# SyncE's order of edge-attribute loads, index loads and waits in the convolution phase of a two-layer graph network

## The reference, cut to what matters

```
filters  = silu(edge_attr @ fW1 + fb1) @ fW2 + fb2      # edge_attr: 206250 x 50
messages = (h[src] @ dW + db) * filters                 # h: layer norm and relu of x, 6250 x 128
aggregated = segment_sum(messages, dst, 6250)
x = x + (h + silu(aggregated @ uW1 + ub1) @ uW2 + ub2)
```

## Time and profile before

| | us |
|---|---|
| median of 3 runs (5270.76 to 5274.32) | 5273.22 |
| the profiled execution, its own time | 5256.96 |
| its span in the trace, first to last instruction | 5255.3 |
| TensorE busy in the span (matmuls) | 3757.2 |
| GpSimd busy | 3117.0 |
| VectorE busy | 2361.3 |
| ScalarE busy | 1582.3 |
| convolution over the edges, start of gathers to start of the node update | 2684 to 5228 |

### The profile page before, as it was taken

How to read it: one execution, slowest core, us unless ns; L and a number is a source line. 1 busy time by engine, 2 the same in 40 slices (tenths; PEclk the granted TensorE clock), 3 DMA queues, 4 the chain that set the end, 5 groups by cost and what they waited for, 6 DMA issues and landing times. The chain is left out here.

```text
span 5255.3 us, 54906 instructions
## 1 busy us (share of the span) xinstructions
PE 3757.2 (71%) x14371; PEld 2737.0 (52%) x14372; DVE 2361.3 (45%) x5579; ACT 1582.3 (30%) x4766; POOL 3117.0 (59%) x3258
## 2 busy tenths in 40 slices
PE   7666666666666666666747767776767677777868
PEld 5444444444444444444546555565655556656656
DVE  6566666666666666666652222222222222222223
ACT  4455445555445555455420010000100100010001
POOL 4666666666666666666455565656556656665653
PEclk9555555555555555555575566656566655565567
DMA  2222222222222222222122222222222222222222
GB/s 79 46 45 45 45 45 44 44 45 45 45 45 44 45 44 45 46 45 44 40 76 58 55 60 59 57 59 61 55 59 59 57 59 60 57 60 59 57 59 62
DMA packets 150585, 277.69 MB, mean 53 GB/s; under 512 B 77209, under 2 KB 91489, under 8 KB 146054
## 3 DMA queue, kind: packets, MB, share of 16 engines
q0 software_dynamic: 104064, 218.11, 17.7%
q1 hardware_dynamic: 46290, 58.74, 4.0%
q10 hardware_dynamic: 200, 0.48, 0.0%
HBM read 267.31 MB, written 9.73 MB: 53 GB/s over the span
## 5 line engine op out<-in xcount | busy, mean ns | idle before, releaser
L57 POOL DMA_INDIRECT ce_xg<-table,ce_idx x1612 | 1527.0, 947 | 1003.2 <-DVE ce_msg L1211 516.2
L57 POOL DMA_INDIRECT ae_xg<-table,ae_idx x1612 | 1538.9, 955 | 936.7 <-issue 467.7
L1138 ACT ACTIVATE ce_hid<-ce_ps_h,ce_fb 128x768 f32<-128x768 f32 x269 | 242.2, 901 | 2288.5 <-remote 1542.5
L1179 PE MATMUL ce_ps_h<-ce_ea,ce_fw 50*128 50x384 f32 x1076 | 669.3, 764 | 322.8 <-ACT ce_hid L1138 168.6
L1208 DVE TENSOR_TENSOR ce_ps_f<-ce_ps_f,ce_fb 128x768 f32<-128x768 f32 x269 | 259.2, 963 | 1409.7 <-remote 1046.4
L1158 PEld LDWEIGHTS ce_ps_f<-ce_fw,ce_hid 128*128 128x128 f32 x3228 | 638.1, 293 | 399.8 <-issue 377.1
L1158 PE MATMUL ce_ps_f<-ce_fw,ce_hid 128*128 128x128 f32 x3228 | 728.3, 397 | 146.6 <-issue 146.1
L654 PE MATMUL ae_ps_k<-ae_xg,ae_e 128*96 128x129 f32 x3224 | 832.2, 430 | 1.1 <-ACT ae_e L567 1.1
L654 PEld LDWEIGHTS ae_ps_k<-ae_xg,ae_e 128*96 128x96 f32 x3224 | 685.4, 278 | 46.8 <-issue 45.5
L1167 PE MATMUL ce_ps_a<-ce_hot,ce_msg 128*128 128x32 f32 x3224 | 569.0, 332 | 194.1 <-issue 193.9
L1167 PEld LDWEIGHTS ce_ps_a<-ce_hot,ce_msg 128*128 128x128 f32 x3224 | 588.2, 272 | 195.2 <-issue 195.1
(11 more groups left out here) (144 smaller groups left out, 3204.2 us busy)
## 6 DMA issues: line engine op xcount, KB each, us to landing
ce_ea<-in_edge_attr SPq DMA_DIRECT2D x90, 450.0 KB
ae_xg<-table,ae_idx POOLq DMA_INDIRECT x1612
ce_xg<-table,ce_idx POOLq DMA_INDIRECT x1612
table<-pr_rows POOLq DMA_DIRECT2D x7, 462.0 KB, 4.1
pr_x<-in_x SPq DMA_DIRECT2D x7, 448.0 KB, 3.3
table<-fa_hd SPq DMA_DIRECT2D x7, 448.0 KB, 3.0
out_x<-y SPq DMA_DIRECT2D x7, 448.0 KB, 3.0
fa_x<-in_x SPq DMA_DIRECT2D x6, 448.0 KB, 4.0
```

Of the source, the lines that this page charges most:

```text
L57: eng.indirect_dma_start(out=out, out_offset=None, in_=table[:, :], in_offset=bass.IndirectOffsetOnAxis(ap=idx, axis=0)).then_inc(done, 16)
L1138: nc.scalar.activation(hid[:, b, :].rearrange("p (k e) -> p k e", k=2), ps_h[:, :].rearrange("p (k e) -> p k e", k=2)[:, :, 0:H], ACT.Silu ...
L1179: last = nc.tensor.matmul(ps_h[:, k * 512:k * 512 + H], fw1[:, :], ea[:, s // LOAD, q:q + H], start=True, stop=True)
```

## The change: what it does

`load_indices` takes a function that issues the attribute load, and calls it at another place and with another turn. Before, load k stood ahead of the wait for the gathers of group k and the index load of group k+2. Now both attribute loads of the first turn stand at the very start, and in each group of turn i the attribute load of turn i+1 follows the index load. So load k+2 comes right behind the wait for the gathers of group k. The last turn issues no attribute load. There are 90 attribute loads and 92 index loads, as before, with the same waits, buffers and sizes. The attention stage calls `load_indices` without the function and issues what it issued before. No other engine's program changes.

```diff
-def load_indices(sp, a, h, idx, idx_in, gathered, landed, also=lambda r, i, v: None):
+def load_indices(sp, a, h, idx, idx_in, gathered, landed, ahead=lambda r, i, v: None):
...
         def following(i):
             for v in range(LOADS):
-                also(r, i, v)
                 read(r, i, v)
                 sp.dma_start(idx[v][:, :],
                              a["src"][bass.ds((i + 1) * LOADS + v, 1), :, 0:P // 2, :].rearrange("u o p c -> (u o) p c")).then_inc(idx_in[v], 16)
-
+                ahead(r, i + 1, v)
+
+        for v in range(LOADS):
+            ahead(r, 0, v)
         following(0)
         with sp.Fori(1, TURNS - 1) as i:
             following(i)
         for v in range(LOADS):
-            also(r, TURNS - 1, v)
             read(r, TURNS - 1, v, REST)
             sp.dma_start(idx[v][:, :], a["src"][v, :, 0:P // 2, :]).then_inc(idx_in[v], 16)
```

## The result

The changed kernel took 5295.01 us (median of 6, 5287.97 to 5303.38), the kernel before on the same chip 5273.77 us (6 runs, 5269.71 to 5279.64). The ratio is 1.0039, interval 1.0028 to 1.0051: 21 us slower. The forecast was 5268 us and no change that can be told; 5295.01 us lies at the upper end of the range (5295).

A forecast was written before the change was run, and what follows sets the result against it. The prediction took the convolution to be paced between GpSimd and TensorE, with SyncE outside that loop. Steady loads 0, index loads 0 and start -5 us turned 5273.2 into 5268 us, range 5239 to 5295.

The forecast's parts named there:

- What bounds the phase: Convolution: no engine full; GpSimd pauses 6.0 us per group for TensorE's chain, 28.14 us per group, no SyncE instruction involved.
- (a): Convolution's attribute loads 2 to 89: 60 go out some 6 us earlier, but nobody waits for them; 0 us.
- bounds of -23 to +43: Best and worst for the steady loads, in us, from stretches of 27.75 and 28.86 us per group over 60 groups.
- the forecast's own sign of being wrong: Convolution's steady pace off 28.14 us by over 0.2 us per group, with GpSimd's pause or its filter-step distance changed.
- 28.24 against 28.14 us per group: Average of 20 earlier groups whose loads already went out early, against the whole steady part; difference taken as 0.
- the longest delay of loads 2 to 87: Convolution: the longest an attribute load went out behind its product's ACT, read as 11.4 us at load 51.
- (b): Convolution's index loads, now behind a later product's wait: 10 us remain in the tightest case; 0 us.
- rival 3: Convolution: GpSimd waits for a delayed index load; 20 groups with 1 us give 5288 us; chance 0.02.
- Just behind the attribute load: Where the changed profile would show the index load in groups like load 30's.
- (c): Convolution's start: load 1 goes out near 2688 instead of 2713.01 us, unit 3 sooner; 0 to 11.1, taken as -5 us.
- Rival 4: Convolution's start gives nothing because TensorE's chain is held back otherwise before unit 3; 5273 us; chance 0.04.
- Rival 2: Slower: earlier transfers and gathers hold each other up, filters come later, GpSimd's pause grows; up to 5311 us; chance 0.17.

The follow-up runs named there:

- e18: Three convolution passes, attribute loads issued by ScalarE behind the silu, SyncE keeping only index loads; against e15: 10365.05 us (-3.5 us).
- e12: The changed kernel repeated, against the kernel before in a set where that took 5268.75 us: ratio 1.0015 (1.0005 to 1.0024).
- e14: Only the steady order changed, start as before, against the kernel before in the set of e11: ratio 1.0011 (1.0001 to 1.0021).
- e11: The kernel before, unchanged, repeated against itself in a set where it took 5268.75 us: ratio 0.9993 (0.9982 to 1.0003).
- e13: Only the start changed (load 1 right behind load 0), against the kernel before in the set of e11: ratio 0.9992 (0.9983 to 1.0001).
- e15: The kernel before with the convolution stage gone through three times, attention once; base of e16 to e18: 10368.56 us.
- e17: Three convolution passes with only the steady order changed, the start of each pass as before; against e15: 10402.43 us (+33.9 us).
- e10: The changed kernel with a 1 MB device-memory copy by ScalarE behind each silu (264 copies); against the kernel before: ratio 1.0102 (1.0057 to 1.0146).
- e8: The changed kernel with each unit's segment-sum matmuls done twice, making TensorE the bound; against e7: 4858.66 us, 19 us faster.
- e16: The changed kernel with three convolution passes, attention once; against e15: 10399.46 us (+30.9 us).
- e9: The kernel before with a 1 MB device-memory copy by ScalarE behind each silu (264 copies); against the kernel before: ratio 1.0065 (1.0027 to 1.0103).
- e1: The kernel before, unchanged, repeated against itself in a set where it took 4307.2 us: ratio 1.0007 (0.9998 to 1.0016).
- e3: Only the start changed (load 1 right behind load 0), against the kernel before in the set of e1: ratio 1.0004 (0.9994 to 1.0015).
- e2: The changed kernel repeated, against the kernel before in the set of e1: ratio 0.9990 (0.9981 to 0.9999).
- e4: Only the steady order changed, start as before, against the kernel before in the set of e1: ratio 0.9992 (0.9983 to 1.0001).
- e7: The kernel before with each unit's segment-sum matmuls done twice, making TensorE the bound; base of e8: 4877.62 us.

## Why the prediction was wrong

- **What bounds the phase**: right for the long sets. GpSimd's pauses of 6 us per group stayed (500 us), and the pace is set between GpSimd and TensorE. It went too far where it concluded from "no attribute buffer or SyncE instruction is in that loop" that SyncE's order has no price. There is no semaphore of SyncE in the loop, but TensorE's own pauses and its granted clock are, and both changed with SyncE's order.
- **(a), the steady loads, 0 us**: the step that failed. The shorter waits were worth nothing, as said, and the transfers' new place too as far as can be told (e18: -3.5 us for three passes). But (a) and (b) together, the new steady order, measured +12 us in e12 and e14 against e11 and e13, about 9 to 11 us for each pass in e15 to e17, and 8 us in the steady part of the result's own trace. That lies inside the bounds of -23 to +43, and the steady pace of 28.24 us is within the 0.2 us that I had allowed, so the forecast's own sign of being wrong did not show there (nor in e12, 28.41 against 28.25 in e11). The average that I had worked out from the earlier trace rows, 28.24 against 28.14 us per group, is 0.1 x 84 = +8 us; I had dismissed just this difference as scatter. That the result has the same 28.24 is luck: those stretches were chosen for early attribute loads, and e18 shows that these do no harm by themselves. One reading was wrong besides: the longest delay of loads 2 to 87 is 30.7 us (load 2), not 11.4 us (load 51). No wait followed from it.
- **Outside the sum**: the forecast put everything outside the convolution at nothing, since no instruction there changes. The two profiled executions have 20.9 of their 35.5 us in the attention stage. Whether the change made them is open, as said below.
- **(b), the index loads, 0 us**: that GpSimd would not wait for them held in every trace without added traffic; with it (e10) there were 39.5 us of such waits, rival 3's mechanism. "Just behind the attribute load" was wrong: 4.7 us behind the ACT (median), because SyncE's instructions between the two loads take that long here (in e8, without pauses, the index load is 1.5 us behind). That this place costs nothing was reasoned from who waits for the load. The runs tie the loss to SyncE's order: e16 and e18 differ in that SyncE's index loads, and what goes with them, stand behind the product's wait, and in the queue of the attribute load. Which of the two it is, no run parts; an early attribute load on SyncE with the index loads elsewhere was not tried.
- **(c), the start, -5 us**: 0 in the result's trace, where unit 3 came 6.3 us sooner (relative to the first gather) and unit 4 0.2 us; the pauses took the rest. e13 against e11 is -2 us by means, within its scatter. Without pauses and with TensorE as the bound it is worth 14 to 19 us (e8). Rival 4 described this case, for another reason.
- **Rival 2** had the right side, at a chance of 0.17, with a mechanism that e18 speaks against: the same early transfers on another queue cost nothing that can be told. The Trainium skill's rule beside it (DMA: Bandwidth & Descriptors, Issuing engines are not separate DMA queues) is not contradicted: sharing the DMA engines had no price here that could be measured, at a DMA share of 0.22 (e18).
- **What stays open.** First, 21 us were measured for the result and about 12 in the set of e11 to e14; the profile of after has 21 us in the attention stage, whose instructions did not change. In all six pairs of profiles of an old and a new steady order in such sets (result, e11 and e12, e13 and e14, e15 and e16, e15 and e17, e9 and e10) the attention stage is longer in the changed one, by 8 to 34 us, while the timed runs of e11 to e17 leave it 3 us, give or take 9. The stage varies without the new order too (2462 to 2478 us in before, e11, e13, e15 and e18, against 2472 to 2488 with it, e9 and e10 left out). One profile for each kernel can't settle it. Second, how SyncE's instructions and TensorE's pauses are tied was only argued from where both lie. The changed order also lays SyncE's program out anew, and no run parts the place of its instructions in the program from the order of its waits. Third, the clock: over all timed runs the mean granted clock of an execution is 0.573 in e11 and e13 and 0.563 and 0.564 in e12 and e14; in the quick set it is 0.609 and 0.610 in e1 and e3 and 0.605 and 0.606 in e2 and e4. It is lower with the new order in both kinds of set (though not in e8 and e10), but where GpSimd is the bound this costs nothing. In the others the filter and hidden products are some 60 us longer for each pass (e16 against e15: 88 and 86 us in three passes). Part of this is absorbed: TensorE waits 47 us less for ScalarE in a pass, while 31 us more of its idle time before the hidden products have no explanation. The table above speaks for the clock and not for the pauses in the filters; a run that holds one and moves the other is missing, so the cause stays open. What is shown is that the loss comes with SyncE's new steady order, and that it is gone when ScalarE issues the same early loads.

No version beats the kernel before in both kinds of set by more than the measurement tells: ScalarE's queue is at 0.9990 in one and at -3.5 us of 10369 in the other.

## What to carry to other kernels

A wait that nobody waits for can still matter by what releases it: an engine that is let go by TensorE's product does all its work at TensorE's next step, in every round. Here the loss came with such an order, though how was not shown. Before an experiment is called a test of a moved load, look in its trace whether the load has moved: in e7 it already stood where e8 puts it. When two things change with a loss, lay all pairs side by side, those without the loss too. And before a change of under 1% is judged, measure it in several sets of runs, with the parts apart.

## What the runs showed of the hardware

- The same kernel took 4307, 4309, 5269, 5273, 5274 and 5406 us as the median of six sets, the result's among them, and chip number 11 gave both 4307 and 5273. Why, no run shows. Attention takes about 2031 us in the quick sets and 2462 to 2595 us in the others.
- The traces of the long sets show engines that start instructions late without a wait. Between the attribute load at 4426.10 and the index load at 4432.44 above SyncE executes three register instructions, a branch and a move, which begin 0.7 to 1.4 us apart; in the quick sets no register instruction of SyncE takes over 0.19 us. TensorE's products at the start begin 2.1, 2.8 or 3.5 us apart. What these are no row names. The Trainium skill (Runtime: NRT & Kernel Launch, Instruction fetch mechanics) says that sequencers fetch their instructions by themselves and that the cost is mostly hidden; the quick traces are in line with this (no pause inside a group), and whether the pauses in the others are such fetches, no run here shows.
- Without pauses the kernel has another bound (GpSimd, 22.5 us per group) than with them (28.2 us per group), and the sign of a small change turned with it (e2 0.9990, e12 1.0015).
- The granted clock of the same products moved with the order of waits on SyncE, which executes no product: 0.573 to 0.563 (e11, e12), 0.589 to 0.576 (e15, e16).
